# Experts that add their weighted rows to the residual in memory, in place of a gather at the end

## The reference

```python
x1 = u + normalize(state_space_layer(normalize(u)))   # the first residual
xf = normalize(x1)
x3 = xf + attention(layernorm(xf)) @ Wproj
flat = layernorm(x3)
gates = softmax(flat @ Wgate)                      # 8 experts
top_inds = top_k(gates, 2)                         # each token picks 2
# an expert takes its first 1024 tokens, in order; later ones are dropped
hmid = gelu(exp_in @ W1 + b1)                      # 256 -> 1024, per expert
exp_out = hmid @ W2 + b2                           # 1024 -> 256
moe[token] += exp_out[expert, slot] * gate         # up to 2 per token
out = x1 + normalize(x3 + moe)
```

## Time and profile before

| | us |
|---|---|
| median of 3 runs | 4218.1 (4218.03 to 4223.59) |
| the profiled execution, span from its first to its last instruction | 4222.2 |
| busy: PE / DVE / ACT / POOL | 3401.3 / 2787.7 / 2464.7 / 1886.3 |
| routing, first to last scatter issue | 3521.0 to 3626.5 |
| experts, first load to last store issue | 3637.3 to 4104.3 |
| combination, first load to end | 4111.7 to 4222.2 |

### The profile page before, as it was taken

One profiled execution on the slowest core, in us unless ns is written; L12 is line 12 of the kernel. 1 busy time (PEld: TensorE's weight loads), 2 busy tenths in 40 slices (PEclk: granted clock), 3 DMA queues, 4 the chain that ended last, 5 costly groups with the idle time before them and its releaser, 6 DMA issues. The chain is left out here.

```text
span 4222.2 us, 69815 instructions
## 1 busy us (share of the span) xinstructions
PE 3401.3 (81%) x22940; PEld 2121.0 (50%) x22940; DVE 2787.7 (66%) x4369; ACT 2464.7 (58%) x3860; POOL 1886.3 (45%) x1761
## 2 busy tenths in 40 slices
PE   8567878878788787885876999999999976599980
PEld 4146666666666666664553333333333335366660
DVE  3258888888888888886764777777777727100105
ACT  3268888888888888884220555665566552122110
POOL 1048888888888888885541000010001015200006
PEclk9679999999999999998995999999999996799995
DMA  6533333333333333334634001011001025122205
GB/s 204 156 101 91 91 91 91 91 91 91 92 91 89 93 91 89 91 93 183 236 119 120 9 19 19 7 19 22 17 9 19 9 64 189 34 83 83 83 31 188
DMA packets 158040, 357.64 MB, mean 85 GB/s; under 512 B 20931, under 2 KB 65974, under 8 KB 143216
## 3 DMA queue, kind: packets, MB, share of 16 engines
q1 hardware_dynamic: 125392, 266.42, 22.8%
q0 software_dynamic: 16784, 52.10, 3.5%
q10 hardware_dynamic: 15504, 34.61, 2.2%
HBM read 253.24 MB, written 102.26 MB: 84 GB/s over the span
## 5 line engine op out<-in xcount | busy, mean ns | idle before, releaser
L506 POOL TENSOR_TENSOR scan_hC<-scan_hh,scan_cbc 128x512 f32<-128x512 f32 x1024 | 1382.8, 1379 | 160.1 <-DVE scan_hh L718 101.4
L718 DVE TENSOR_TENSOR_SCAN scan_hh<-scan_dA,scan_state,scan_bx 128x512 f32<-128x512 f32 x1024 | 1252.4, 1264 | 213.9 <-PE scan_bx L810 99.5
L810 PE MATMUL scan_bx<-kept_ident,scan_dBxT 128*128 128x128 f32 x4096 | 677.3, 292 | 197.5 <-DVE scan_hh L718 133.5
L1561 PE MATMUL attend_s<-attend_kt,attend_qt 32*128 32x512 f32 (+3 forms) x2560 | 793.7, 609 | 33.9 <-DMA attend_qt<-attend_zero 27.6
L559 ACT ACTIVATE scan_dBxT<-scan_dtxT,scan_bt 128x512 f32<-128x512 f32 x1028 | 655.7, 711 | 81.6 <-PE scan_bx L810 81.4
L820 PE MATMUL scan_acc<-kept_ident,scan_hC 128*128 128x128 f32 x4128 | 656.8, 287 | 56.1 <-ACT scan_uu L568 29.3
L810 PEld LDWEIGHTS scan_bx<-kept_ident,scan_dBxT 128*128 128x128 f32 x4096 | 502.4, 150 | 389.7 <-DVE scan_hh L718 232.1
L554 ACT ACTIVATE scan_dA<-scan_dt,scan_an 128x512 f32<-128x512 f32 x1028 | 660.9, 712 | 29.1 <-DVE scan_hh L718 29.1
L1582 PE MATMUL attend_s<-attend_qt,attend_kt 32*128 32x512 f32 (+3 forms) x2560 | 635.7, 581 | 17.9 <-POOL attend_pb L1438 14.6
L1472 DVE TENSOR_REDUCE attend_mx<-attend_s 128x1 f32<-128x512 f32 x768 | 494.5, 686 | 197.0 <-PE attend_s L1561 195.8
L1532 ACT ACTIVATE attend_pb<-attend_s 128x1024 f32<-128x1024 f32 x384 | 390.8, 1024 | 279.1 <-PE attend_s L1582 279.1
(11 more groups left out here) (207 smaller groups left out, 3675.1 us busy)
## 6 DMA issues: line engine op xcount, KB each, us to landing
scan_xs<-scratch_xin SPq DMA_DIRECT2D x288, 256.0 KB, 6.2
scan_cbc<-scratch_crows SPq DMA_DIRECT2D x64, 1024.0 KB, 4.8
scratch_y<-scan_uu ACTq DMA_DIRECT2D x17, 1024.0 KB
scratch_xin<-proj_out_x SPq DMA_DIRECT2D x8, 1024.0 KB
scratch_sz<-proj_out_z SPq DMA_DIRECT2D x8, 1024.0 KB
scratch_exp_in<-proj_cleared SPq DMA_DIRECT2D x8, 1024.0 KB, 8.4
mix_yf<-scratch_y SPq DMA_DIRECT2D x8, 1024.0 KB, 6.6
mix_yb<-scratch_y SPq DMA_DIRECT2D x8, 1024.0 KB, 9.5
```

What stands on the lines that cost most here:

```text
L506: pool.tensor_tensor(hC[n % 2][:, m, :], h[:, m, :], rows, ALU.mult).then_inc(hc_ok, 1)
L718: dve.tensor_tensor_scan(hh[n % 2][:, m, r], dA[n % 2][:, m, r], bx[bank(j)][:, r], state[:, d, n, m:m + 1], ALU.mult, ALU.add).then_inc(h ...
L810: last = pe.transpose(bx[bank(j)][:, t * P:(t + 1) * P], dBxT[turned_slot(n)][:, t, m * P:(m + 1) * P], k["ident"][:, :])
L1561: pe.matmul(s1[v % S1][:, 0:w], qt[n % SETS][rows, t * P:(t + 1) * P], kt_[n % SETS][rows, c * C:c * C + w], start=True, stop=True).then_i ...
```

## The change

A row of `exp_in` grows from 256 to 261 numbers (1044 bytes): the token's index, its two chosen experts and their two weights come behind the 256. Routing fills them in h (the scatter carries them along) and no longer keeps slots and gates on chip. Unfilled slots are initialized with zeros as before, but with a token index of their own behind the last token; x3 in memory gets 1024 spare rows for them.

In the experts DVE reads the extra columns of an expert's rows: the index becomes the offset, and the weight that belongs to this expert is picked. After the bias it multiplies each tile by the weight of its rows. POOL adds each tile of 128 rows to x3 in memory by an indirect transfer that accumulates, eight per expert, and waits for all of one expert before the next. `exp_out` is gone. SP loads all of x1 to the chip behind the rows of expert 1. PE waits for the biased tile (`b_ok`), the rest for the weighted one (`y_ok`).

The combination loads all eight chunks of x3 at once into eight buffers, without waits between, normalizes each, and adds x1: POOL for even chunks, DVE for odd ones. DVE measures chunk n + 1 before it normalizes chunk n. SP stores. The list is written out instead of looped. The stages that hold the weights and routing inputs now close after the combination rather than before it.

```diff
+ROW = D + 5
+TOKEN, PICK, WEIGH = D, D + 1, D + 3
+SPARE = CAP
...
-        CLEARED = E * CAP * D // (B * NC * P)
-        cleared = s.sb("cleared", [P, CLEARED])
+        CLEARED = E * CAP // (B * NC * P)
+        cleared = s.sb("cleared", [P, CLEARED, ROW])
+        spares = s.sb("spares", [P, CLEARED])
...
             sp.dma_start(w[:, :, :], in_wT.rearrange("(k p) m -> p k m", p=P)).then_inc(loaded_w, 16)
-            sp.wait_ge(zeroed, 2)
+            sp.dma_start(spares[:, :], spare).then_inc(loaded_spares, 16)
+            sp.wait_ge(zeroed, 3)
...
-                    sp.dma_start(slots_view[t], cleared[:, :]).then_inc(clears, 16)
+                    sp.dma_start(slots_view[t], cleared[:, :, :].rearrange("p r d -> p (r d)")).then_inc(clears, 16)
...
-            pool.memset(cleared[:, :], 0.0).then_inc(zeroed, 1)
+            pool.memset(cleared[:, :, :], 0.0).then_inc(zeroed, 1)
+            pool.wait_ge(loaded_spares, 16)
+            pool.wait_ge(zeroed, 2)
+            pool.tensor_copy(cleared[:, :, TOKEN], spares[:, :]).then_inc(zeroed, 1)
...
-        ht = [s.sb(f"ht{i}", [P, JT, D]) for i in range(4)]
+        ht = [s.sb(f"ht{i}", [P, JT, ROW]) for i in range(4)]
+        tokens = s.sb("tokens", [P, NTOK // P])
...
+            sp.dma_start(tokens[:, :], token).then_inc(loaded_t, 16)
...
-                    last = dve.tensor_scalar(h[:, j, :], x3t[n % 3][:, j, :], mv[i][:, j, 0:1], rstd[i][:, j:j + 1],
+                    last = dve.tensor_scalar(h[:, j, 0:D], x3t[n % 3][:, j, :], mv[i][:, j, 0:1], rstd[i][:, j:j + 1],
...
+                if t == 0:
+                    dve.wait_ge(loaded_t, 16)
+                h = ht[t % 4]
+                dve.tensor_copy(h[:, :, TOKEN], tokens[:, t * JT:(t + 1) * JT])
+                dve.tensor_copy(h[:, :, PICK:PICK + 2], chosen[:, :, :])
+                dve.tensor_copy(h[:, :, WEIGH:WEIGH + 2], top[:, :, 0:2]).then_inc(slot_ok, 1)
...
+                dve.wait_ge(slot_ok, t + 1)
                 dve.scalar_tensor_tensor(out=send[t % 2][:, :, :], in0=over[:, :, :], scalar=BIG_SLOT,
                                          in1=slot_f[:, :, :], op0=ALU.mult, op1=ALU.add).then_inc(send_ok, 1)
-                at4 = slice(t * JT, (t + 1) * JT)
-                dve.tensor_copy(slots[:, at4, :], slot_f[:, :, :]).then_inc(slot_ok, 1)
-                dve.tensor_scalar(clipped[:, :, :], over[:, :, :], -1.0, 1.0, ALU.mult, ALU.add
-                                  ).then_inc(slot_ok, 1)
-                dve.wait_ge(slot_ok, t * 3 + 2)
-                dve.tensor_tensor(gates[:, at4, :], top[:, :, 0:2], clipped[:, :, :], ALU.mult).then_inc(slot_ok, 1)
-                dve.wait_ge(slot_ok, t * 3 + 3)
...
-        xt = [s.sb(f"xt{i}", [P, ST, D]) for i in range(2)]
+        xt = [s.sb(f"xt{i}", [P, ST, ROW]) for i in range(2)]
+        idx = [s.sb(f"idx{i}", [P, ST], I32) for i in range(2)]
+        share = [s.sb(f"share{i}", [P, 2, ST]) for i in range(2)]
+        gate = [s.sb(f"gate{i}", [P, ST]) for i in range(2)]
...
+                if e == 1:
+                    for n in range(B * NC):
+                        sp.dma_start(x1t[n][:, :, :], x1v[n // NC, n % NC]).then_inc(loaded_x1, 16)
+            sp.wait_ge(loaded_x1, 16 * B * NC)
...
             for e in range(E):
+                if e:
+                    for ch in range(CH):
+                        pool.wait_ge(added[ch], 16 * JT * e)
                 for ch in range(CH):
-                    pool.wait_ge(y_ok, e * ST + (ch + 1) * JT)
-                    hold(pool, k)
-                    pool.dma_start(yv[e, ch], yt[ch][:, :, :]).then_inc(stored[ch], 16)
+                    for j in range(JT):
+                        at = ch * JT + j
+                        pool.wait_ge(y_ok, e * ST + at + 1)
+                        hold(pool, k)
+                        pool.indirect_dma_start(
+                            out=x3, out_offset=bass.IndirectOffsetOnAxis(ap=idx[e % 2][:, at:at + 1], axis=0),
+                            in_=yt[ch][:, j, :], in_offset=None, bounds_check=NTOK + SPARE - 1, oob_is_err=True,
+                            compute_op=ALU.add).then_inc(added[ch], 16)
             for ch in range(CH):
-                pool.wait_ge(stored[ch], 16 * E)
+                pool.wait_ge(added[ch], 16 * JT * E)
...
+            def read_rows(e):
+                own, i = xt[e % 2], e % 2
+                if e >= 2:
+                    for ch in range(CH):
+                        dve.wait_ge(added[ch], (e - 1) * JT * 16)
+                dve.tensor_copy(idx[i][:, :], own[:, :, TOKEN])
+                for w in range(2):
+                    last = dve.scalar_tensor_tensor(out=share[i][:, w, :], in0=own[:, :, PICK + w], scalar=float(e),
+                                                    in1=own[:, :, WEIGH + w], op0=ALU.is_equal, op1=ALU.mult)
+                last.then_inc(share_ok, 1)
+                dve.wait_ge(share_ok, e + 1)
+                dve.tensor_tensor(gate[i][:, :], share[i][:, 0, :], share[i][:, 1, :], ALU.add).then_inc(meta_ok, 1)
+
+            def weigh(e, j):
+                own = yt[j // JT][:, j % JT, :]
+                dve.wait_ge(b_ok, e * ST + j + 1)
+                dve.tensor_scalar(own, own, gate[e % 2][:, j:j + 1], None, ALU.mult).then_inc(y_ok, 1)
+
             copy_turned(0)
+            read_rows(0)
             for e in range(E):
                 if e + 1 < E:
                     copy_turned(e + 1)
+                dve.wait_ge(meta_ok, e + 1)
                 for j in range(ST):
                     if j % JT == 0 and e:
-                        dve.wait_ge(stored[j // JT], e * 16)
+                        dve.wait_ge(added[j // JT], e * 16 * JT)
                     dve.wait_ge(y_mm, e * ST + j + 1)
                     dve.tensor_tensor(yt[j // JT][:, j % JT, :], py[j % 2][:, :], b2t[e % 2][:, :], ALU.add
-                                      ).then_inc(y_ok, 1)
+                                      ).then_inc(b_ok, 1)
+                    if j:
+                        weigh(e, j - 1)
+                weigh(e, ST - 1)
+                if e + 1 < E:
+                    read_rows(e + 1)
...
-                        pe.wait_ge(y_ok, e * ST + j - 1)
+                        pe.wait_ge(b_ok, e * ST + j - 1)
...
-def combine(nc, k, exp_out, slots, gates, x3, x1, out):
...
+def combine(nc, k, x3, x1t, out):
+    LAST = B * NC
     with Stage(nc, "combine") as s:
+        x3t = [s.sb(f"x3t{i}", [P, JT, D]) for i in range(LAST)]
+        stats = [s.sb(f"stats{i}", [P, JT, 6]) for i in range(2)]
+        mv = [s.sb(f"mv{i}", [P, JT, 2]) for i in range(2)]
+        rstd = [s.sb(f"rstd{i}", [P, JT]) for i in range(2)]
+        loaded = s.sems(*[f"loaded{i}" for i in range(LAST)])
+        (st_ok, mv_ok, log_ok, rstd_ok, n_ok, sum_even, sum_odd, stored) = s.sems(
+            "st_ok", "mv_ok", "log_ok", "rstd_ok", "n_ok", "sum_even", "sum_odd", "stored")
+        x3v, ov = tok_view(x3[0:NTOK, :]), tok_view(out)
         block = s.block()
         @block.sync
         def _(sp):
+            for n in range(LAST):
+                sp.dma_start(x3t[n][:, :, :], x3v[n // NC, n % NC]).then_inc(loaded[n], 16)
+            for n in range(LAST):
+                if n % 2 == 0:
+                    sp.wait_ge(sum_even, n // 2 + 1)
+                else:
+                    sp.wait_ge(sum_odd, n // 2 + 1)
+                sp.dma_start(ov[n // NC, n % NC], x3t[n][:, :, :]).then_inc(stored, 16)
+            sp.wait_ge(stored, 16 * LAST)
         @block.gpsimd
         def _(pool):
+            for n in range(0, LAST, 2):
+                pool.wait_ge(n_ok, n + 1)
+                pool.tensor_tensor(x3t[n][:, :, :], x3t[n][:, :, :], x1t[n][:, :, :], ALU.add).then_inc(sum_even, 1)
         @block.vector
         def _(dve):
+            def measure(n):
+                i = n % 2
+                dve.wait_ge(loaded[n], 16)
                 for j in range(JT):
+                    last = dve.bn_stats(stats[i][:, j, :], x3t[n][:, j, :])
+                last.then_inc(st_ok, 1)
+                dve.wait_ge(st_ok, n + 1)
+                if n >= 2:
+                    dve.wait_ge(rstd_ok, n - 1)
                 for j in range(JT):
+                    last = dve.bn_aggr(mv[i][:, j, :], stats[i][:, j, :])
+                last.then_inc(mv_ok, 1)
+            def normalize(n):
+                i = n % 2
+                dve.wait_ge(rstd_ok, n + 1)
                 for j in range(JT):
+                    last = dve.tensor_scalar(x3t[n][:, j, :], x3t[n][:, j, :], mv[i][:, j, 0:1], rstd[i][:, j:j + 1],
                                              ALU.subtract, ALU.mult)
                 last.then_inc(n_ok, 1)
+                if n % 2:
+                    dve.wait_ge(n_ok, n + 1)
+                    dve.tensor_tensor(x3t[n][:, :, :], x3t[n][:, :, :], x1t[n][:, :, :], ALU.add
+                                      ).then_inc(sum_odd, 1)
+            measure(0)
+            for n in range(LAST):
```

(68 more changed lines are left out.)

76 lines of the change are left out of this document (15 added, 61 removed).

## The result

The changed kernel took 4160.0 us (median of four runs, 4155.0 to 4162.3), the kernel before 4219.3 (four runs, 4218.0 to 4223.6): a ratio of 0.9855, 95% interval 0.9842 to 0.9867, so 59.3 us less. Between the two profiled executions it is 4222.2 to 4159.2, 63.0 us; the four runs of either kernel spread over 6 and 7 us.

What follows compares the result with a forecast made beforehand. The last stage was taken as bound by POOL issuing gathers, the experts by PE. Last stage -67.7, seam +4.1, steps 1 to 3 +1.6 gave -62.0 us, so 4156, range 4144 to 4180.

Steps and rivals of the forecast that it cites:

- Step 1: Kernel start: POOL waits for and copies the spare-row table before the first x load; +1.7 us (0 to +3.9).
- Step 2: Routing: three small operations and their waits go, three copies come in; -0.6 us (-2.7 to +4.1).
- Step 3: First expert load, which PE waits for: longer, odd-sized rows cost +0.5 us.
- Step 4: Experts: DVE's weighing and POOL's 64 accumulating scatters are covered by PE; cost 0.
- Step 5: Seam from experts to last stage: the last scatters must land before the first load; +4.1 us (+1.7 to +8.5).
- Step 6: Last stage: gathers and scale-and-add go, leaving mostly DVE's work; 110.5 to 42.8 us, first load to end.
- the feared price of odd-sized rows: First expert load: a third more time for odd-sized rows, 1.9 us; +0.5 taken for the load.
- Rival C: Experts: accumulating scatters bound them, making the kernel slower from 7.6 us per scatter; 4369 at 10 us; 8%.
- B: Experts and seam: scatters back up partly, lengthening the seam past 3.5 us each, up to +29 us, 4185; 7%.
- A: Last stage: bound by its 16 transfers of 512 KB; time 4165 to 4177; 9%.
- D: Whole change: straight-line last stage or waits between experts eat the gain, no change in time; 3%.
- The hold by POOL: Last stage: POOL's additions of even chunks make DVE's normalizations wait; 1 us taken, 0 to 2.

Runs made afterwards that it cites:

- experiment 1: Kernel before with only its last stage rewritten (no loop, all loads at once, own buffers), the 64 gathers kept: 4218.3 us against 4224.6, ratio 0.9991.
- Experiment 2: Changed kernel with every accumulating scatter issued two or four times, the extra ones to scratch arrays nobody reads: 4161.0 us with two, 4238.4 with four.
- Experiment 6: Changed kernel with the copy of the spare indices moved from POOL to ACT, so POOL issues the x loads at once: 4149.7 us.
- Experiments 4 and 5: 4: changed kernel with routing's three old operations and two waits put back, routing 141.4 us; 5: kernel before, unedited, profiled again, routing 140.7 us.
- experiment 3: Changed kernel with all eight additions of x1 on DVE and none on POOL: 4168.0 us.

## Why the prediction was right

It said -62.0 us and 4156 (4144 to 4180); measured -59.3 and 4160.0. By its steps (each read from the two profiles, routing from all):

| step | predicted | measured |
|---|---|---|
| 1 start | +1.7 (0 to +3.9) | +5.1 |
| 2 routing | -0.6 (-2.7 to +4.1) | -1.0 |
| 3 first expert load | +0.5 | -0.3 |
| 4 experts | 0 | 0 |
| 5 seam | +4.1 (+1.7 to +8.5) | +3.3 |
| 6 last stage | -67.7 | -67.8 |
| sum | -62.0 | -60.7 |

The sum is near because the last stage gives more than the whole gain and came out as priced, itself with some luck (step 6). The errors of the small steps, +3.4 in the start and -2.0 in steps 2, 3 and 5, partly cancel; that is luck too. The 2.3 us between this sum and the 63.0 of the two profiles lie in routing's stalls and attention (step 2) and in stages that the change leaves alone.

**What bounded the kernel** was named rightly: experiment 1 kept the gathers and changed the loop, the buffers and the loads, and the time stayed. Experiment 2 shows why the scatters are free where they were put: POOL had the room for twice as many.

**Step 1 was mis-sized**, outside its bounds. The issue time was 0.7 us off (10.03, against 9.3); the landing was further off, 6.6 us in place of 3.9. The prediction reasoned that the wires would be free by then. The weights were gone, but the step didn't list what else is queued behind the new wait: SP's four stores of zeros also wait for the copied table (`zeroed`, 3), and two of them moved from just behind the x loads to just ahead of them. Experiment 6 shows the wait; that the slower load comes from those stores is argued there.

**Step 2 was right, though the two profiles alone said otherwise.** Between them routing is 8.4 us shorter (148.3 to 139.95), outside the bounds. Experiments 4 and 5 put 7.6 of that (148.3 - 140.7) down to stalls of one execution of before. What hid this in the total: attention was 8.4 us longer in the profile of the change (1199.7 us from its first to its last score product before, 1208.1 after), with a granted clock of 0.96 and 0.97 in two 250-us stretches (2753 to 3253) where before had 0.99. Other executions, of kernels with either list, show 0.95 to 0.99 there; in them attention took 1205.0 and 1206.6 us with the old list and 1203.0 to 1209.0 with the new, so the first profile of before was the odd one. Two differences of 8 us, neither made by the change, nearly cancelled.

**Step 3**: the experts' first load took 5.4 us (3640.88 to 3646.31) with the longer rows, against 5.7; the feared price of odd-sized rows isn't there. In all executions it was 5.3 to 5.5 with 1044-byte rows and 5.7 to 5.9 with 1024; why, no run tells.

**Step 4**, with PE's group in the experts of the kernel after: the weighing took 0.34 us (0.41 assumed) and PE's second-layer products waited for nothing:

```profile
L2194 PE MATMUL experts_py<-weights_w2t,experts_hid 128*128 128x256 f32 x1024 | 222.3, 379 | 0.0
```

Rival C put its turning point at 7.6 us a scatter and B at 3.5: 1.86 was measured, with the queue full.

**Step 5**: the landing was 3.8, not 5.8; the last scatter began 0.7 us later behind the last add than assumed (3.4 against 2.7), mostly because a scatter costs 1.86 and not 1.3 in the queue; and the closing took 4.5 instead of 4.0, though two stages fewer close there, since POOL's DRAIN took 2.99 us in place of 1.36. Together -0.8: two misses took back part of the third.

**Step 6** came out at 42.7 us where 42.8 was worked out, by luck: errors of opposite sign. Hand-overs of 0.25 us a chunk, 2 in all, weren't there: DVE's operations follow each other without a gap. Statistics, aggregates and normalizations alone took 24.4 us (experiment 3: 34.2 less 9.8 for the additions) where the groups' sum gave 25.5. From DVE's last addition to the end it was 6.1 us where 5.5 was taken; the 0.7 in it for two stores that share the wires is a term that no run shows by itself. The hold by POOL was 3.6 us where 1 was taken and 2 was the bound. Three normalizations behind a POOL addition took 1.90 instead of 1.35, 0.55 each, as estimated; the fourth took 1.96 more, since behind chunk 6 no statistics are left to run under POOL's addition (the pair of 4.66 above). The loop was priced by its middle and not by its end.

The Trainium skill (SBUF — State Buffer, "Who interferes with whom") has it that a VectorE operation in a two-port mode, or a two-input one beside a GpSimd operation that reads SBUF, waits when the GpSimd operation was issued first. Experiment 3 agrees for the normalization (401 ns against 514 on the mean); statistics beside the same addition kept their 1.40.

**Rivals.** A: DVE never waited for a load after the first (and 359 GB/s was not the best rate: the trace of before has 418 from 6 to 7 us, so 20 us of transfers rather than 23). B and C: 256 additions at 1.86 us each, with no growth, are far from both turning points (C's 213 us at s = 10 should read 216: 3687.8 + 640 less 4111.8). D: the time rules it out; experiment 1 shows that the rewrite alone, without the scatters, would have done nothing.

## What to carry to other kernels

A gather at the end, where nothing runs beside it, may be turned into accumulating scatters inside a stage that another engine bounds; what counts is how much idle time the issuing engine has there, and here it had room for twice the work. When a wait is added to one engine, list what every other engine has queued behind the same semaphore: here four small stores changed their place before the load that all wait for, and that load took 2.0 us longer on top of the wait. Compare two profiled executions stage by stage, and profile the old kernel twice before a difference that no edit explains is given to the change.

## What was not expected of the hardware

- A scatter of 128 rows of 1 KB holds POOL 0.98 us, an accumulating one 1.56, and they land after 2.4 and 3.8 us; one behind the other, the accumulating ones start 1.86 us apart.
- The first x load took 4.5 us behind the weights and 6.3 to 7.1 where two small stores were issued ahead of it. In its first two microseconds a 4 KB packet held a DMA engine for 0.66 us on the mean, later for 0.16. Why stays open.
- POOL's DRAIN at the end of the experts took 1.35 to 5.28 us, and stood on the path to the next stage's first load: 1.36 after plain stores, 2.99 after accumulating scatters, 5.28 after plain ones.
- A DVE operation on four elements per partition took 0.13 us alone and up to 1.50 beside a POOL addition.
- DVE stalls of 18.5 us in seven places, marked remote, in one execution of a program and in none of another of the same program. Their cause stays open.
